# A four-layer graph network: gated turns in pairs, the last two groups side by side

## The reference

```python
def reference(x, adj, ...):                    # x: (64, 256, 128), adj: (256, 256) of 0 and 1
    # layer 0: attention masked by adj
    A = exp(8 * tanh((x @ q) @ (x @ k).T / sqrt(128) / 8)) * adj
    x = layernorm(x + (A / A.sum(-1)) @ x @ v)
    # layer 1: five steps of a gated recurrent network on h = x
    for _ in range(5):
        m = adj @ h                            # both message matrices are adj here
        av = concat(m, m)
        u3 = h @ u3_w.T + u3_b
        z = sigmoid(av @ w3_w.T + w3_b + u3)
        r = sigmoid(av @ w4_w.T + w4_b + u3)
        hv = tanh(av @ w5_w.T + w5_b + (r * h) @ u5_w.T + u5_b)
        h = (1 - z) * h + z * hv
    x = layernorm(x + h)
    # layer 2: powers 0 to 3 of adj, each with its weights
    x = layernorm(x + sum(power_k(adj) @ x @ w_k))
    # layer 3: messages
    f = relu(x @ psi_w + psi_b)
    msg = (adj * adj).T @ f
    hid = relu(concat(msg, x) @ phi1_w + phi1_b)
    x = layernorm(x + hid @ phi2_w + phi2_b)
```

## Time and profile before

| | us |
|---|---|
| median of 3 runs | 1379.63 |
| lowest and highest | 1378.92 and 1381.86 |
| the profiled execution | 1379.54 |
| its span, first to last instruction | 1377.8 |

### The profile page before, as it was taken

One profiled execution on the slowest core, in us unless ns is written; L12 is line 12 of the kernel. 1 busy time (PEld: TensorE's weight loads), 2 busy tenths in 40 slices (PEclk: granted clock), 3 DMA queues, 4 the chain that ended last, 5 costly groups with the idle time before them and its releaser, 6 DMA issues.

```text
span 1377.8 us, 27560 instructions
## 1 busy us (share of the span) xinstructions
PE 1337.2 (97%) x8630; PEld 1186.4 (86%) x8630; DVE 1081.9 (79%) x2537; ACT 950.3 (69%) x1730; POOL 861.8 (63%) x907
## 2 busy tenths in 40 slices
PE   8999979999999999999999999999899999999995
PEld 6999967888888888888888888887689999999994
DVE  4788857777778777787777787777788888888885
ACT  4888857776777777777776777766546666666664
POOL 5988866666666666666666666665435555555554
PEclk9999999999999999999999999999999999999998
DMA  3233322000020000020000110000212222222211
GB/s 105 86 100 106 95 100 77 1 0 0 15 85 24 0 0 0 32 89 0 0 0 0 54 39 1 0 0 10 76 54 70 70 69 69 69 69 69 69 39 39
DMA packets 60048, 61.25 MB, mean 44 GB/s; under 512 B 4690, under 2 KB 39380, under 8 KB 59988
## 3 DMA queue, kind: packets, MB, share of 16 engines
q1 hardware_dynamic: 59556, 60.31, 13.9%
q10 hardware_dynamic: 432, 0.20, 0.1%
HBM read 35.33 MB, written 25.17 MB: 44 GB/s over the span
## 4 chain that ended last, share of the span: by engine, by line
PE 91%; DVE 4%; ACT 2%; POOL 2%; issue 1%; DMA 0%; ACTq 0%; POOLq 0%; DVEq 0%
PE psum L1039 6%; PE psum L733 5%; PE psum L735 5%; PE psum L721 5%; PE psum L382 4%; PE psum L1051 3%; PE psum L1053 3%; PE psum L776 3%; PE psum L765 3%; PE psum L748 3%; PE psum L777 3%; PE psum L746 3%; PE psum L778 3%; PE psum L766 3%; PE psum L768 3%; PE psum L769 3%
## 5 line engine op out<-in xcount | busy, mean ns | idle before, releaser
L696 POOL TENSOR_TENSOR rh_lo<-rh,rh_hi 128x512 fp32r<-128x512 f32 x160 | 207.0, 1294 | 264.3 <-ACT rh_hi L811 264.3
L702 POOL TENSOR_TENSOR h_lo<-h,h_hi 128x512 fp32r<-128x512 f32 x160 | 216.6, 1354 | 12.8
L811 ACT CAST rh_hi<-rh 128x512 fp32r<-128x512 f32 x160 | 99.4, 621 | 147.8 <-DVE rh L843 147.8
L824 DVE TENSOR_TENSOR psum<-psum,h 128x512 f32<-128x512 f32 x160 | 111.9, 699 | 102.4 <-ACT psum L815 102.4
L733 PE MATMUL psum<-adj_t_hi,hn_hi 128*128 128x256 f32 x640 | 172.6, 303 | 1.0 <-DVE m_lo L837 1.0
L808 ACT ACTIVATE psum<-psum,bias_cols 128x512 f32<-128x512 f32 x160 | 106.7, 667 | 79.2 <-PE psum L753 79.0
L735 PE MATMUL psum<-adj_t_hi,hn_lo 128*128 128x256 f32 x640 | 159.2, 283 | 0.0
L843 DVE TENSOR_TENSOR rh<-psum,h 128x512 f32<-128x512 f32 x160 | 110.1, 688 | 50.8 <-ACT psum L808 50.7
L733 PEld LDWEIGHTS psum<-adj_t_hi,hn_hi 128*128 128x128 f32 x640 | 122.2, 191 | 2.0 <-issue 2.0
L735 PEld LDWEIGHTS psum<-adj_t_hi,hn_lo 128*128 128x128 f32 x640 | 122.5, 191 | 0.0
L798 ACT ACTIVATE z<-psum,bias_cols 128x512 f32<-128x512 f32 x160 | 111.2, 695 | 0.0
(11 more groups left out here) (197 smaller groups left out, 4341.6 us busy)
## 6 DMA issues: line engine op xcount, KB each, us to landing
x_in<-in_x_dram SPq DMA_DIRECT2D x32, 256.0 KB, 3.0
x_dram<-x SPq DMA_DIRECT2D x32, 256.0 KB, 2.1
g_x<-x_dram SPq DMA_DIRECT2D x32, 256.0 KB, 3.1
h_dram<-h SPq DMA_DIRECT2D x32, 256.0 KB, 2.0
ht<-h_dram SPq DMA_DIRECT2D x32, 256.0 KB, 2.8
c_x<-x_dram SPq DMA_DIRECT2D x32, 256.0 KB, 3.1
out_dram<-res SPq DMA_DIRECT2D x32, 256.0 KB, 2.4
conv_in<-in_L_gnn_weight_dram SPq DMA_DIRECT2D x1, 448.0 KB, 4.8
```

What stands on the lines that cost most here:

```text
L696: pool.tensor_tensor(rh_lo[:, q, :], rh[:, q, :], rh_hi[:, q, :].bitcast(F32), ALU.subtract).then_inc(rh_lo_done, 1)
L702: pool.tensor_tensor(h_lo[:, q, :], h[:, (g - 1) % G, :], h_hi[:, q, :].bitcast(F32), ALU.subtract).then_inc(h_lo_done, 1)
L824: dve.tensor_tensor(cb, cb, hg, ALU.subtract).then_inc(dif_done, 1)
```

## The change

In the gated layer, slots 8 to 151 (`paired`) are taken in twos: TensorE turns the groups of both slots at the start of the even one, the second into bank 7 (`B_HN_ODD`), and the odd slot has no turn. The turn waits for the last reader of its own bank. ScalarE and VectorE read the bank through `hn_bank`.

In the last pipeline the engines write out two slots more after the loop (slots 32 and 33, `L_W`) and then a `drain` of their own, in which groups 30 and 31 go through the message layer side by side. Group 31 gets places of its own for x3t, the parts of its features and messages, its hidden layer and its sums, in tiles and banks that are free by then. The moments are summed for one norm at a time (`combine`, four columns). `idle_products` issues matmuls whose result nobody reads, five while x3 of group 31 is made and three before the last outputs. The last result is written by ScalarE (one tile) and by VectorE (three tiles, which need no `shift`). The core of both parts:

```diff
+    def paired(base, g):
+        return not isinstance(base, int) or G <= base + g < SLOTS - G
+    def hn_bank(base, g):
+        return B_HN_ODD if paired(base, g) and g % 2 else B_HN
...
     def tensor(pe):
+        def turn(base, g, k, bank):
+            s = base + g
+            if k is not None:
+                pe.wait_ge(x1_loaded[g], k * 16 + 16)
+            else:
+                pe.wait_ge(h_done, s - G + 1)
+            wait_count(pe, hn_lo_done, s - 1 if paired(base, g) and g > 0 else s)
...
+            for i in range(TILES):
+                src = x1[:, g, i, :] if k is not None else h[:, g, i * 128:(i + 1) * 128]
+                mm = pe.transpose(psum[:, bank, i * 128:(i + 1) * 128], src, ident[:, :])
+            mm.then_inc(hn_mm, 1)
...
+            if not paired(base, g):
+                if live(base, g, 0):
+                    turn(base, g, k, B_HN)
+            elif g % 2 == 0:
+                turn(base, g, k, B_HN)
+                turn(base, g + 1, k, B_HN_ODD)
...
@@ tensor of the last pipeline
+        def drain():
+            pe.wait_ge(hid_done, LAST - 1)
+            features(B_F, x3t, LAST - 1)
+            idle_products(5)
+            pe.wait_ge(x3_done, GROUPS)
+            pe.wait_ge(y1_done, GROUPS)
+            for i in range(TILES):
+                mm = pe.transpose(psum[:, B_T1, cols(i)], x3[:, LAST % 4, i, :], ident[:, :])
+            mm.then_inc(x3t_mm, 1)
+            pe.wait_ge(c_lo_done[1], GROUPS)
+            messages(NEXT_MSG, f_hi, f_lo, LAST - 1)
+            features(END_F, end_x3t, LAST)
+            hidden_of_x3(B_F, x3t_hi[:, :], x3t_lo[:, :], LAST - 1)
+            hidden_of_message(B_F, msg_hi[:, :], msg_lo[:, :], LAST - 1)
+            pe.wait_ge(c_lo_done[2], GROUPS)
+            messages(END_MSG, end_f_hi, end_f_lo, LAST)
+            pe.wait_ge(y3_done, LAST - 1)
+            outputs(B_M, hid, LAST - 1)
+            pe.wait_ge(y2_done, GROUPS)
+            hidden_of_x3(END_HID, end_x3t_hi, end_x3t_lo, LAST)
+            hidden_of_message(END_HID, end_msg_hi, end_msg_lo, LAST)
+            idle_products(3)
+            outputs(END_O, end_hid, LAST)
@@ scalar
+            turned(x3t[:, :], B_T23, LAST - 1)
+            result(LAST - 3, every)
+            act.wait_ge(msg_mm, LAST - 1)
+            features_hi(f_hi[:, :, :], B_F, LAST - 1)
+            act.wait_ge(y1_done, GROUPS)
+            turned(end_x3t, B_T1, LAST)
+            message_hi(msg_hi[:, :], NEXT_MSG, LAST - 1)
+            act.wait_ge(a_mm[2], GROUPS)
+            features_hi(end_f_hi, END_F, LAST)
+            act.wait_ge(o_mm, LAST - 1)
+            hidden(hid[:, :], B_F, LAST - 1)
+            message_hi(end_msg_hi, END_MSG, LAST)
+            result(LAST - 2, every)
+            hidden(end_hid, END_HID, LAST)
+            result(LAST - 1, every)
+            result(LAST, every[:1])
@@ vector
+            combine(ln1, 0, ENTRY + 1)
+            dve.wait_ge(rstd_x3_done, GROUPS)
...
+            op.then_inc(x3_done, 1)
+            features_lo(f_lo[:, :, :], f_hi[:, :, :], B_F, LAST - 1)
+            sum_with_x3(B_M, LAST - 2)
+            message_lo(msg_lo[:, :], msg_hi[:, :], NEXT_MSG, LAST - 1)
+            features_lo(end_f_lo, end_f_hi, END_F, LAST)
+            combine(ln2, 0, ENTRY + 2)
+            message_lo(end_msg_lo, end_msg_hi, END_MSG, LAST)
+            sum_with_x3(B_M, LAST - 1)
+            combine(ln2, 1, ENTRY + 3)
+            sum_with_x3(END_O, LAST)
+            combine(ln2, 0, ENTRY + 4)
+            dve.wait_ge(rstd_done, LAST + L_Y3 + 1)
...
+            op.then_inc(res_half_done, 1)
@@ gpsimd
+            x3_with_bias(LAST - 1)
+            ln1 = slice(LN1 * TILES, BATCH)
+            pool.wait_ge(var_done, ENTRY + 1)
+            pool.tensor_tensor(rstd[:, 0, ln1], var_eps[:, 0, ln1], minus_half[:, ln1], ALU.pow).then_inc(rstd_x3_done, 1)
+            pool.wait_ge(x3_done, GROUPS)
+            halves_of_x3(x3t[:, :], x3t_hi[:, :], x3t_lo[:, :], LAST - 1)
+            halves_of_x3(end_x3t, end_x3t_hi, end_x3t_lo, LAST)
+            last_power(LAST - 2, ENTRY + 2)
+            x3_with_bias(LAST)
+            last_power(LAST - 1, ENTRY + 3)
+            last_power(LAST, ENTRY + 4)
```

More of the change, by code:

```diff
@@ L611, in gated_layer @@
     z = sb("z", [128, 2, COLS])
-    B_HN, B_M, B_R, B_GATE = 0, 1, 2, 4
+    B_HN, B_M, B_R, B_GATE, B_HN_ODD = 0, 1, 2, 4, 7
     B_CAND = (3, 6)
@@ L948, in run @@
                     second(it, u)
-        for u in range(lags):
-            slot(GROUPS // U + u // U, u % U)
+        for u in range(L_W):
+            slot(GROUPS // U, u)
     def live(it, u, lag):
@@ L998, in slot @@
                 sp.dma_start(out_view[:, bass.ds(n * TILES, TILES), :], res[:, u % 2, :, :]).then_inc(res_out[u % 2], 16)
-        yield from run(sp, slot, L_RES)
+        yield from run(sp, slot)
+        for n in range(GROUPS - 4, GROUPS):
+            sp.wait_ge(res_done, n + 1)
+            if n == LAST:
+                sp.wait_ge(res_half_done, 1)
+            sp.dma_start(out_view[:, n * TILES:(n + 1) * TILES, :], res[:, n % 2, :, :]).then_inc(res_out[n % 2], 16)
         for i in range(2):
@@ L1156, in slot, with features @@
                 mm.then_inc(x3t_mm, 1)
-        yield from run(pe, slot, L_F)
+        def features(bank, src, n):
+            pe.wait_ge(x3t_done, n + 1)
+            pe.matmul(psum[:, bank, :], ones[:, :], flat(psi_row[:, :, :]), start=True, stop=False, skip_group_check=True)
+            for i in range(TILES):
+                mm = pe.matmul(psum[:, bank, cols(i)], src[:, cols(i)], psi[:, :], start=False, stop=True,
+                               skip_group_check=True)
+            mm.then_inc(f_mm, 1)
@@ new lines, in messages @@
+        def messages(bank, hi, lo, n):
+            pe.wait_ge(f_lo_done, n + 1)
+            for b in range(GB):
+                dst = psum[:, bank, :].rearrange("p (c b n) -> p c b n", c=KC, b=GB)[:, :, b, :]
+                for k in range(KC):
+                    pe.matmul(dst, hi[:, tile(b, k), :], adj_sq[:, k, :], start=(b == 0 and k == 0), stop=False,
+                              skip_group_check=True)
+                    mm = pe.matmul(dst, lo[:, tile(b, k), :], adj_sq[:, k, :], start=False, stop=(k == KC - 1),
+                                   skip_group_check=True)
+            mm.then_inc(msg_mm, 1)
@@ L1159, in scalar @@
+        yield from run(pe, slot)
+        drain()
     def scalar(act):
@@ L1310, in graph_conv_layers @@
+        yield from run(dve, slot)
+        drain()
     return {"sync": sync, "gpsimd": gpsimd, "tensor": tensor, "scalar": scalar, "vector": vector}
```

153 lines of the change are left out of this document (131 added, 22 removed).

## The result

| | before | changed |
|---|---|---|
| median of 6 runs, us | 1379.39 | 1368.20 |
| lowest and highest | 1378.91 and 1381.86 | 1365.76 and 1370.52 |
| the profiled execution, and its span | 1379.54, 1377.8 | 1365.86, 1364.1 |

The ratio is 0.9913 (95% interval 0.9899 to 0.9927): 12 us or 0.9% faster by it, 11.2 by the medians. The forecast was 4.1, and the lower end of its range was 1372.9. The direction was right; the size was not.

What follows compares the result with a forecast made beforehand. TensorE was taken to bound the loops and the chain of hand-overs the last 38 us. 1379.54 - 4.6 (end) + 0.6 (pairs) gave 1375.5 us, with 1372.9 to 1377.8 for 8 in 10.

Steps and rivals of the forecast that it cites:

- the gain on TensorE itself is 0: Gated stage: pairing moves transposes, removes none, and a change of kind costs nothing, so TensorE gains 0.
- its bound of 2.9: Gated stage: if all slots became like the shorter or longer neighbour, 72 x 0.04 = 2.9 us would go or come.
- the end: Last pipeline: groups 30 and 31 side by side and a shared last result, -4.6 us, bounds -5.6 and -3.0.
- pairs gain: Rival, gated stage: the 0.04 between neighbouring slots goes, 2.9 more in place of the 0.6, 1372.0 to 1372.6; 10%.
- +0.6 for the first steps: First step of sets 1 to 3, gated stage: pairs lose 0.2 more in each, 3 x 0.2; bounds 0 and +1.3.
- the cover of 4.43 for a loop of 4.42: Gated steps reading h: 4.43 from even to odd gates just fits the 4.42 VectorE and ScalarE loop; no TensorE wait.
- the bound (-5.6): End, best case: result 29 in time (0.3) and sums over 4 columns in place of 12 shorter (0.7).
- 1363.5 and 1363.8: End, ScalarE's queue: sums for hid of 31 come near 1363.5, result 29 ahead of it ends at 1363.8.
- half: Rival, end: two passes sharing ScalarE's and VectorE's fixed order hold each other up, only -2.3, 1377.8; 18%.
- The clock did not fall: Rival, gated stage: eight transposes in a row lower the granted clock; one fall in each of 18 passes costs 31, 1406; 4%.
- The second turn's h: Rival, gated stage: the second turn finds its h unfinished and TensorE stands, despite three slots of slack; 1%.
- the marks set: Wrong if two slots take under 9.65 or over 9.8, the clock falls (223 to 940), or hid of 31 waits elsewhere.

Runs made afterwards that it cites:

- e6_behind: Kernel before with single turns in one bank, one per slot, placed behind the slot's messages; 1383.14 beside 1379.22 us (one run).
- e1: Kernel before with the turns in pairs alone, old end; 1373.38 against 1379.49 us, ratio 0.9959.
- e3: Kernel before with the two banks and looser wait, but a turn of four transposes in each slot; 1380.82 beside 1379.49 us (one run).
- e4: Kernel before with both turns in the even slot, the second behind the messages, old end; 1376.01 beside 1379.49 us (one run).
- e5: Kernel before with every turn in slots 8 to 151 done twice, eight transposes per slot; 1432.70 beside 1379.22 us (one run).
- e2_end: Kernel before with the new end alone, turns one by one; 1372.97 against 1379.49 us, ratio 0.9953.

## Why the prediction was right or wrong

**Wrong: "the gain on TensorE itself is 0", and its bound of 2.9.** This step carries most of the miss: the gated stage was forecast at +0.6 and measured -6.2, while the end was off by 0.7. It had two halves. That a change of kind costs nothing holds (0.554 + 0.556 before, 0.992 + 0.118 after). The other half was silent: that with no cost at the border of a group, nothing else could change. I measured the matmuls behind a group of four from one pair of slots and took 0.233 and 0.118 for what they cost. They were not at their floor: that slot was of the longer kind, at the longer spacing throughout, and with the pairs the 15 products of a slot take 3.434 and not 3.502 or 3.459.

The bound failed in the same way. I did see 4.88 and 4.84 and called the 0.04 unexplained; I bounded it by making every slot like the shorter, 0.02 a slot on the average. But the shorter slot was no floor, it had 0.04 in it still. All quick, two slots take 9.60, 0.12 less, three times the bound. The rival "pairs gain", 10%, had the right sign and the right row, and was sized by the same mistake. The trace of before held the answer: in set 2, behind a step in which TensorE waits, come slots of 623.85 - 619.03 = 4.82 and 628.64 - 623.85 = 4.79:

```profile
619.03 0.60 PE L721 MATMUL psum<-ident,h 128*128 128x128 f32 x4
...
623.85 0.60 PE L721 MATMUL psum<-ident,h 128*128 128x128 f32 x4
...
628.64 0.60 PE L721 MATMUL psum<-ident,h 128*128 128x128 f32 x4
```

Two like the last are 9.58. I had read one stretch of two slots, when the spread over 144 was to be had.

The sum with the right term: 60 pairs in steps that read h at -0.12 is -7.2; three first steps at +0.18 is +0.5; together -6.7. From slot 8 to slot 152 the traces have 702.33 and 696.07, -6.3; the 0.4 between is mostly before's: behind the first steps of sets 1 and 2 its two slots took 9.61 (the 4.82 and 4.79 above are those of set 2), so there was 0.11 less to gain in each, and the rest is in single slots.

**Right: +0.6 for the first steps.** It measured +0.5, by the way that was written (three times 0.18 for 3 x 0.2). The loop through VectorE and ScalarE sets that step, and e6_behind shows it from the other side: a later turn costs there at once.

**Right in the outcome, not in the figures: the cover of 4.43 for a loop of 4.42.** In the steps that read h two slots are 9.60 in 59 of 60 pairs, with no wait of TensorE in them. But with the quicker matmuls the cover is 4.37, the length of an odd slot, and under the 4.42 that the loop was given. The loop made it, because its part from rh to L840 (L824 of before) took 1.94 and not the 2.01 of the earlier trace rows:

```profile
647.06 0.69 DVE L859 TENSOR_TENSOR rh<-psum,h 128x512 f32<-128x512 f32 x1 [0.76 <-ACT psum L824]
...
649.00 0.70 DVE L840 TENSOR_TENSOR psum<-psum,h 128x512 f32<-128x512 f32 x1 [0.65 <-ACT psum L831]
```

**Right in its mechanism, small in its size: the end.** The chain went as written, and each step behind the moments came a little earlier:

| from the moments, us | forecast | measured |
|---|---|---|
| power begins | 2.0 | 1.78 |
| x3 of 31 begins | 3.1 | 2.83 |
| f_lo of 30 begins | 4.2 | 3.86 |
| messages of 30 begin | 5.0 | 4.69 |
| features of 31 begin | 6.0 | 5.71 |
| power for 29 begins | 9.7 | 9.20 |
| result 29 begins | 11.0 | 10.52 |
| hid of 31 begins | 12.6 | 12.08 |
| y3 of 31 begins | 14.5 | 13.99 |
| last power begins | 17.2 | 16.49 |
| last store issued | 19.2 | 18.47 |

0.2 is gone with the first step already, and another 0.2 between y3 and the last power: 2.50 for 2.73. Both hold moments and sums, 1.78 and 1.77 from the start of the moments to the power in place of 2.01. I had named the sums over four columns as part of the bound (-5.6) and not of the value. But they are only 0.06 shorter (0.87 for the 0.93 of the earlier trace rows). The other 0.17 lies between the moments and the first sum, where the old slot has four waits for semaphores and the new order one; no run separates that. A third 0.2 is in features of 31 to the power for 29, 3.49 for 3.73: the sums for 29 stand behind f_lo on VectorE itself, 2.63 behind the start of the features, and the 2.80 of the forecast ran to TensorE's messages. ScalarE's hid of 31 begins right behind result 29 (1353.36 + 1.66), and TensorE's sums for it end at 1354.46 + 0.39 = 1354.85: a tie, as near as "1363.5 and 1363.8" had it. Which of the two holds it was not separated.

**Not foreseen: the clock in the old end.** The old end took 37.31 to 37.35 in three traces and 38.37 to 38.39 in five (e1, e3, e4, e5, e6), in all five with a fall of the granted clock during TensorE's work like the one shown. The new end took 31.98 to 32.02 in four traces, with a fall behind the last product only. A mean over the eight old ends is 38.0, so the new end is worth 0.65 more than the profiled pair shows, which is in line with the 6.5 that e2_end measured. The forecast had looked at the earlier trace rows, saw 1.00 from 1352 to 1370, and took one execution for all.

**The rivals.** The end gave all and more, so "half" is out. The clock did not fall between 223 and 932. The second turn's h was always ready. By the marks set: two slots under 9.65 were to show me wrong, and did. The upper end of the forecast's own band, 1377.5, is not what its bounds give: 1379.54 - 3.0 + 1.3 = 1377.8.

**What stays open.** Why a group of six leaves the matmuls behind it at the long spacing, four at a mixed one and eight at the short. Bank and wait are excluded (e3_banks), and a shared rhythm with the other engines is unlikely, since slots of 4.80, 4.84, 4.88, 5.10 and 5.23 fall into the same few sums. That would leave TensorE itself or how its instructions reach it, which no run tested. The weight loads start at the same two spacings as the matmuls, so the traces don't tell which of them follows the other.

## What to carry to other kernels

Where an engine is full, start-to-start spacings of the same instruction over the whole stage are worth a view of their own: two values for one form (0.2335 and 0.2289 here) can be a gain that is open to a mere reordering, and the floor to reckon with is the least that any stretch shows, not the lesser of two neighbours. At 97% TensorE, 0.12 us in two slots is 7 us in the kernel. In an end of hand-overs, write the chain out with the durations of its new shapes, and take the clock of several executions, since one can miss a fall that most have.

## What the runs showed of the hardware

The spacing of float32r matmuls, each with its own weights, is not one number: 15 of 512 columns took 3.434, 3.459 or 3.502 us, at a granted clock of 1.00, by the number of transposes ahead of them and whether messages stood between. These are two spacings, 229 and 233 ns, and for 256 columns 113 and 118 ns. The Trainium skill, "TensorE: Matmul & The Clock Gate", section "Back-to-back issue gap", gives for an isolated matmul the columns by 2.4 GHz and 2.5 ns more, which is 216 ns for 512 columns, and about 131 ns in a stream of weight loads and matmuls; it names no number format there. The trace agrees with neither figure, and the trace shows two spacings where that section has one for each case.

Eight transposes in a row, 0.87 us of each 9.60, left the clock at 1.00 over 709 us. The Trainium skill, "TensorE: Matmul & The Clock Gate", section "Part 4: PE-mode transpose", has it that a transpose doesn't lift the clock as a matmul does. The trace is no test of that, as it has 46 other matmuls around every eight; it shows that this share of them does no harm.

In the first 200 us, near 1000 and in the old end the granted clock was 1.2 GHz for a few us in some traces and not in others, over the same instructions. The four traces without a fall near 19 us reached the first turn at 174.87 to 175.20, the nine with one at 176.05 to 178.59; the first eight slots took 50.92 to 50.95 us in the three without a fall near 190, and 51.90 to 52.04 in the nine others that have the same instructions there. The runs of before ranged from 1376.62 at a mean clock of 0.997 to 1383.42 at 0.989 on one chip, so the spread between its runs goes with such falls.
